# A home per quarter for the projection weight, late weights' pieces behind the normalised heads, and the last rows' slices dealt out anew

## The chip, the cores and the metric

One core of a Trainium2 chip runs one program of some 27,700 instructions. The metric is device time in microseconds (us), the median over the runs. The engines are TensorE (PE; its weight loads are shown as PEld), VectorE (DVE), ScalarE (ACT), GpSimd (POOL) and SyncE (SP), which issues the transfers (DMA).

## The reference, cut to what matters

Two transformer layers over 16 sequences of 128 rows and 512 features. The stretch that the change touches is the second layer's attention and the passage from it to the last feed-forward part.

```
def _L1_xattn_ref(hidden_states, cond, ...):      # 16 query heads, 8 key/value heads of 128
    ln_out = _ln(hidden_states, ln_w, ln_b)
    q  = _ln(_fp8_linear_pertensor(ln_out, wq, ...).reshape(b, s, g, hpg, d), ...)
    k  = _ln(_fp8_linear_pertensor(ln_out, wk, ...).reshape(b, s, g, d), ...)
    v  = _fp8_linear_pertensor(ln_out, wv, ...).reshape(b, s, g, d)
    core = _gqa(q, k, v).reshape(b, s, nh * d)
    qx = _ln(_fp8_linear_pertensor(ln_out, wqx, ...), ...)
    kx, vx = jnp.split(jnp.einsum('bsi,oi->bso', cond, w_kv_x), 2, axis=-1)
    xout = _gqa(qx, _ln(kx, ...), vx).reshape(b, s, nh * d)
    catq = _div_clamp_fp8(jnp.concatenate([core, xout], axis=-1), proj_smooth)
    return jnp.einsum('bsi,oi->bso', catq, wproj) * (proj_in_scale * proj_w_scale)

x = x + jnp.tanh(g_xattn[1]) * _L1_xattn_ref(_layernorm(x), ctx_2048, ...)
x = x + jnp.tanh(g_ffn[1]) * _L1_ffn_ref(_layernorm(x), ...)
```

## The kernel before

The attention of the second layer is a software pipeline of 64 tiles: four quarters of the heads (4 query heads, 4 cross query heads, 2 + 2 key and value heads) times 16 sequences (B = 16). Tile m belongs to quarter m // 16. All engines walk the same steps i from 0 to 63 (`step(i, par, quarter)`), each in its own fixed order, and meet by semaphores. A step does the projections of tile i + 1, the turning, scores and maxima around tile i, the softmax and the attention of tile i - 1, the fp8 rounding of tile i - 2 and the output projection of tile i - 3. Most steps of quarters 2 and 3 run in a hardware loop; the others are written out, so that extra work can be placed in them by number.

TensorE in a step: `keys_values` (L2517, L2518), `context_keys_values` (L99 to L101), `turn_probs` (L2589), half of the output projection with the weight `wp` (L2603), `turn` of the normalised heads (L2568), the other half, `attend`, `scores` (L2579; its second half waits until the residual of tile i - 3 has been added, since both use bank 5) and `queries`.

VectorE in a step: `maxima` (L2875), `probabilities` (L2882, L2884), the sums of squares (L2835), the first half of the fp8 rounding (L1299 to L1303), `normalise_b` (L2839, heads that TensorE then turns), `probs_low` (L2857), `sums_a` (L2831), the second rounding half, `residual` (L2898), `values_low` (L2847), `normalise_a`. ScalarE: exponentials (L2734), squares, probabilities out, `heads_out` (L2755 to L2761), `values` (L2717), `scaled_out` (L2772). GpSimd makes the reciprocal roots (L2482) between the sums of squares and `normalise_b`.

Three side jobs ride on the steps.

The **projection weight** of a quarter (8 x 512 columns) comes as fp32 to a spare slot and is cast to fp16 on ScalarE in four pieces (L2680, `wproj_part`) in step 16q + 2. There is one home for it (`wp`, 8 KB at 122 KB), so the first cast waits until the quarter before has done its last output.

The **late weights**: of the four quarters' projection weights, eight slices are centred and split into high and low parts while attention runs. Slice n is summed and centred on VectorE in step 8 + 3n (an opened step: `late.sums` L233, `late.means` L240, `late.centre_heads` L248), its high parts are made on ScalarE in the next step (L257, L261), its low parts on VectorE in the one after (a split step: `late.lo_segs` L269, `late.lo_plain` L274). SP loads two slices in step 7, after all of the last rows' slices are rounded, and one more with each that is done:

```
            if i == LATE_FIRST - 1:
                sp.wait_ge(sh.q_in, C * KT)
                late.load(sp, 0)
                late.load(sp, 1)
```

The **last rows**: the normalised rows of the last four sequences still have to be scaled on ScalarE (16 pieces, L1696, `rows_part`, dealt out by `ROW_PIECES`) and rounded on VectorE in four slices of 2048 columns (L1810 to L1816, `sh.rounded`), each at the end of the step after the one that `LAST_ROWS` names; SP then stores the slice (L1882).

Of the kernel before, what the change touches and what calls it, by code (L numbers as in the profile page):

```python
# [16 lines left out]
F32R = mybir.dt.float32r  # L17
# [8 lines left out]
P = 128  # L26
B = 16
# [1858 lines left out]
class Dense:  # L1886
# [10 lines left out]
    def __init__(self, nc, env, ctx, mem, home, late, wp_in, a_ps, e_in, x_in, mhalf):  # L1897
# [3 lines left out]
        def at(name, kb, shape, dt=FP32):  # L1901
            return mem.at("d_" + name, kb, shape, dt)
# [3 lines left out]
        for name, hi, lo, n in (("gate1", 149, 147, P), ("up", spare, spare + 8, D), ("down", 139, 131, D),  # L1906
                                ("expert", kv, kv + 8, D)):
            self.raw[name] = at("raw_" + name, lo, [P, KT, n])
            self.w[name] = [at(f"{name}_hi", hi, [P, KT, n], F32R), at(f"{name}_lo", lo, [P, KT, n], F32R)]
        self.hi, self.lo = ([at(f"xT_{n}{c}", kb + 8 * i, [P, KT, CW], F32R) for c, kb in enumerate((kvx, wq, wqx, 64))]  # L1910
                            for i, n in enumerate(("hi", "lo")))
        even = at("xn0", 151, [P, J, D])
# [361 lines left out]
def attention(nc, env, ctx, mem, ready, late, sh):  # L2274
# [10 lines left out]
    def sb(name, kb, shape, dt=FP32):  # L2285
        return mem.at(n_ + name, kb, shape, dt)
# [17 lines left out]
    cq = [sb(f"cq{i}", 118 + 2 * i, [P, KH, P], F16) for i in range(2)]  # L2304
    wp = sb("wp", 122, [P, 8, D], F16)
    c_hi = sb("c_hi", 164, [P, KT, P], F32R)
# [25 lines left out]

    LAST_ROWS = (1, 3, 4, 5)
    ROW_PIECES = {1: range(0, 3), 2: range(3, 4), 3: range(4, 6), 4: range(6, 9), 5: range(9, 12), 6: range(12, 16)}
    de = Dense(nc, env, ctx, mem, homes[Q - 1], late, wp_in, a_ps, e_in, x_in, mhalf)
# [174 lines left out]
    def tensor(pe):  # L2510
# [89 lines left out]

        def output_heads(par, heads):
            for h in heads:
                last = nc.tensor.matmul(bank[5][:], cq[par][:, h, :], wp[:, h, :], start=h == 0, stop=h == KH - 1)  # L2603
            return last

        def output_begin(m, par, read, quarter):
            if opens(m):
                pe.wait_ge(wp_in, m // B * 2 + 2)
            pe.wait_ge(cq_in, m * 2 + 2)
            pe.wait_ge(ex_in, read)  # L2610
            if later(m, 1):
                pe.wait_ge(x_in, m)
            output_heads(par, range(QH))

        def output_end(m, par):
            output_heads(par, range(QH, KH)).then_inc(pj_ps, 1)

        def output(m, par, read, quarter):
            output_begin(m, par, read, quarter)
            output_end(m, par)  # L2620

        def step(i, par, quarter):
# [9 lines left out]
            if has(i - 3):  # L2632
                output_end(i - 3, 1 - par)
            if has(i - 1):
# [37 lines left out]
    def scalar(act):  # L2672
        def wproj(quarter, part):
            i, a = divmod(part, 2)
            if quarter and part == 0:
                act.wait_ge(pj_ps, quarter * B)
            if part == 0:
                act.wait_ge(wraw_in, quarter * 16 + 16)
            raw = slots32[homes[quarter][SPARE]]
            last = nc.scalar.activation(wp[:, 4 * i + 2 * a:4 * i + 2 * a + 2, :], raw[:, i, 2 * a:2 * a + 2, :], ACT.Copy)  # L2680
            if a:
                last.then_inc(wp_in, 1)
# [7 lines left out]
        def wproj_part(i, part):  # L2690
            if isinstance(i, int) and i % B == 2 and i < M:
                wproj(i // B, part)

# [134 lines left out]
    def vector(dve):  # L2828
# [71 lines left out]
        def step(i, par, quarter):  # L2900
# [15 lines left out]
            if number(i) == M - 2:  # L2916
                de.normalise(dve, 0, range(2, J))
            if opened is not None:
                late.means(dve, opened)
                late.centre_heads(dve, opened, 0)  # L2920
            if split is not None:
                late.lo_segs(dve, split, late.SEGS[2:4])
            if has(i):
# [3 lines left out]
            if has(i + 1):  # L2927
                sums_a(i + 1)
            if not later(i, 1):
                sh.rounded(dve, C - 2, KT - 1)  # L2930
# [261 lines left out]
```

## Time and profile before

| | us |
|---|---|
| median of three runs | 1635.4 (1634.8 to 1638.3) |
| profiled execution | 1630.85 |
| its span | 1629.1 |
| TensorE busy in the span | 1574.2 (97%) |
| VectorE, ScalarE, GpSimd busy | 1150.1, 1015.2, 486.0 |
| share of TensorE in the chain that ended last | 71% |

The span is the time from the first to the last instruction of one profiled execution. Durations in the rows come from this execution. Matmuls overlap one another, so a busy share near 100% says that there is no hole, not that the engine does all it could.

### The profile page before, as it was taken

How to read it: one execution, taken by the hardware profiler on the slowest of the kernel's cores; microseconds unless marked ns; L12 is line 12 of the kernel's file. 1: busy time of each engine (PE TensorE's matmuls, PEld its weight loads, DVE VectorE, ACT ScalarE, POOL GpSimd, SP SyncE). 2: the span in 40 equal slices, each digit the busy share in tenths (PEclk: the TensorE clock that was granted, in tenths of full speed). 3: DMA queues.
4: the chain of work that ended last, by engine and by line, in shares of the span. 5: the costliest groups of instructions: out<-in, count | busy, mean ns of one | idle time of the engine just before them, and what ended most of it. 6: DMA issues, size and time to landing. Idle time of an engine off the chain costs nothing.

```text
span 1629.1 us, 27708 instructions
## 1 busy us (share of the span) xinstructions
PE 1574.2 (97%) x9392; PEld 1221.4 (75%) x9392; DVE 1150.1 (71%) x2380; ACT 1015.2 (62%) x2855; POOL 486.0 (30%) x515
## 2 busy tenths in 40 slices
PE   7989979999998999999999999999999999999998
PEld 6878766666777767777777777777777777777887
DVE  6358865444997778888888887677777777898322
ACT  4354335553467877877878777777777777875100
POOL 1000222223524333443333443433443343420000
PEclk9999989999999999999999999999999999999999
DMA  8030648885663232364243353121152121110011
GB/s 304 27 109 28 229 167 271 274 270 175 215 228 124 75 135 79 101 237 143 81 136 99 106 199 116 46 77 58 46 201 66 46 109 58 46 39 7 22 38 39
DMA packets 75813, 196.62 MB, mean 121 GB/s; under 512 B 6896, under 2 KB 27376, under 8 KB 69168
## 3 DMA queue, kind: packets, MB, share of 16 engines
q1 hardware_dynamic: 70016, 176.50, 31.6%
q0 software_dynamic: 5680, 18.62, 3.9%
q8 instruction: 67, 1.10, 0.3%
q14 instruction: 50, 0.41, 0.1%
HBM read 147.12 MB, written 47.97 MB: 120 GB/s over the span
## 4 chain that ended last, share of the span: by engine, by line
PE 71%; DVE 8%; ACT 5%; DMA 1%; issue 1%; POOL 1%; SPq 0%; POOLq 0%; ACTq 0%; DVEq 0%
PE bank L2518 9%; PE bank L2517 9%; PE bank L99 8%; PE bank L101 8%; PE bank L100 8%; PE bank L2579 6%; PE bank L2603 5%; PE bank L2568 4%; PE bank L1423 4%; PE bank L1443 4%; PE bank L2589 3%; ACT t_sc L2734 2%; POOL t_rs L2482 1%; PE bank L1403 1%; DVE x_res L1782 1%
## 5 line engine op out<-in xcount | busy, mean ns | idle before, releaser
L2517 PE MATMUL bank<-t_half,t_xh 128*128 128x256 f16 (+1 forms) x1024 | 309.3, 326 | 0.7 <-DVE t_hn L2839 0.7
L2518 PE MATMUL bank<-t_half,t_xh 128*128 128x256 f16 (+1 forms) x1024 | 306.0, 326 | 0.0
L2479 POOL TENSOR_SCALAR t_ve<-t_ss 128x4 f32<-128x4 f32 (+1 forms) x128 | 25.6, 200 | 580.0 <-DVE t_ss L2835 554.4
L2734 ACT ACTIVATE t_sc<-bank,t_mx 128x128 f32<-128x128 f32 x512 | 180.1, 386 | 17.7 <-DVE t_mx L2875 13.1
L2839 DVE TENSOR_TENSOR t_hn<-bank,t_rs 128x256 f32<-128x256 f32 (+1 forms) x256 | 130.0, 549 | 63.4 <-POOL t_rs L2482 63.4
L2482 POOL TENSOR_TENSOR t_rs<-t_ve,t_mhalf 128x4 f32<-128x4 f32 (+1 forms) x128 | 171.0, 1336 | 10.7
L2517 PEld LDWEIGHTS bank<-t_half,t_xh 128*128 128x128 f16 x1024 | 100.3, 98 | 66.7 <-issue 1.4
L2518 PEld LDWEIGHTS bank<-t_half,t_xh 128*128 128x128 f16 x1024 | 100.2, 98 | 66.0
L2772 ACT ACTIVATE t_y<-bank,smooth 128x128 bf16<-128x128 f32 x512 | 139.3, 401 | 2.3 <-DVE t_cq L1303 2.3
L2603 PE MATMUL bank<-t_wp,t_cq 128*128 128x512 f16 x512 | 130.7, 379 | 0.0
L2579 PE MATMUL bank<-t_hT 128*128 128x128 f32 x1024 | 126.2, 276 | 2.7 <-ACT t_hT L2761 2.3
L2579 PEld LDWEIGHTS bank<-t_hT 128*128 128x128 f32 x1024 | 120.0, 192 | 3.8 <-ACT t_hT L2761 2.8
L2734 ACT ACTIVATION_READ_ACCUMULATOR t_sc<-bank,t_mx 128x1 f32 x512 | 115.4, 225 | 0.0
L2568 PE MATMUL bank<-ident,t_hn 128*128 128x128 f32 x768 | 98.3, 274 | 13.9 <-DVE t_hn L2839 13.8
L2568 PEld LDWEIGHTS bank<-ident,t_hn 128*128 128x128 f32 x768 | 87.3, 140 | 30.0 <-DVE t_hn L2839 18.2
L99 PE MATMUL bank<-t_slot,t_c_hi 128*128 128x512 f32 x256 | 106.3, 415 | 1.3 <-DVE x_res L1771 1.3
L101 PE MATMUL bank<-t_slot,t_c_lo 128*128 128x512 f32 x256 | 101.0, 394 | 0.0
L100 PE MATMUL bank<-t_slot,t_c_hi 128*128 128x512 f32 x256 | 99.6, 389 | 0.0
L2761 ACT ACTIVATE t_hT<-bank,q_wb 128x512 f32<-128x512 f32 x128 | 92.8, 782 | 10.3 <-PE bank L2568 10.2
L2470 POOL TENSOR_SCALAR t_c_hi<-t_cr 128x512 fp32r<-128x512 f32 x63 | 95.0, 1507 | 7.1 <-issue 1.4
L2710 ACT ACTIVATE t_sqk<-bank 128x256 f32<-128x256 f32 x64 | 25.3, 395 | 110.8 <-PE bank L101 110.8
L2884 DVE TENSOR_TENSOR t_sc<-t_sc,t_ri 128x512 f32<-128x512 f32 x128 | 88.5, 692 | 4.4
(355 smaller groups left out, 3878.7 us busy)
## 6 DMA issues: line engine op xcount, KB each, us to landing
t_xh<-xq_scratch SPq DMA_DIRECT2D x64, 512.0 KB, 3.5
t_cr<-in_ctxT_dram SPq DMA_DIRECT2D x64, 256.0 KB, 2.7
t_half<-w_half SPq DMA_DIRECT2D x12, 1024.0 KB, 7.6
y_rows<-s_y SPq DMA_DIRECT2D x39, 256.0 KB, 2.4
e_w<-in_w_units_dram SPq DMA_DIRECT2D x8, 1024.0 KB, 11.8
w_rows<-in_w_qkv_dram SPq DMA_DIRECT2D x8, 1024.0 KB, 5.6
xq_scratch<-z_xs SPq DMA_DIRECT2D x16, 512.0 KB, 3.3
t_slot<-w_plain SPq DMA_DIRECT2D x4, 2048.0 KB, 8.4
```

The lines of the kernel that those rows point to most:

```text
L99: nc.tensor.matmul(out, a_hi, b_hi, start=first, stop=False)
L100: nc.tensor.matmul(out, a_hi, b_lo, start=False, stop=False)
L101: return nc.tensor.matmul(out, a_lo, b_hi, start=False, stop=last)
L2482: nc.gpsimd.tensor_tensor(rs[:, lo:hi], ve[:, lo:hi], mhalf[:, lo:hi], ALU.pow).then_inc(rs_in, 1)
L2517: nc.tensor.matmul(out, rows[:, k, kind, :], w[0][:, k, a:b], start=k == 0, stop=False)
L2518: last = nc.tensor.matmul(out, rows[:, k, kind, :], w[1][:, k, a:b], start=False, stop=k == KT - 1)
L2568: last = nc.tensor.transpose(b3[out][:, n, :], hn[:, h, :], env.ident[:])
L2579: last = nc.tensor.matmul(b3[4 + part][:, h, :], hT[:, (1 - part) * QH + h, :], hT[:, KH + (1 - part) * QG + h // 2, :], start=True, stop= ...
L2603: last = nc.tensor.matmul(bank[5][:], cq[par][:, h, :], wp[:, h, :], start=h == 0, stop=h == KH - 1)
L2734: last = nc.scalar.activation(sc[:, h, :], b3[4 + part][:, n, :], ACT.Exp, bias=mx[:, h:h + 1], accum_out=sm[:, h:h + 1])
L2772: nc.scalar.activation(y[:, part, ramp(h)], b3[6 + part][:, h, :], ACT.Copy, scale=env.smooth8[:, n:n + 1]).then_inc(y_in, 1)
L2839: nc.vector.tensor_tensor(hn[:, lo:hi, :], b3[bk][:, 0:hi - lo, :], rs[:, lo:hi].unsqueeze(2).broadcast_to([P, hi - lo, P]), ALU.mult).the ...
```

## The change

The cast projection weight gets a home in each quarter: the upper half of that quarter's query weight slot, whose lower half alone is used by the fp16 weight. The low part of one of the last stage's inputs, which had lain in that upper half, moves to where `wp` was, another moves a little. The wait for the previous quarter's last output goes, and the four casts are done two by two in steps 16q + 1 and 16q + 2. The last rows' pieces are dealt out over steps 1 to 7 instead of 1 to 6, and their roundings end steps 3, 4, 6 and 7 instead of 2, 4, 5 and 6. On VectorE the late weights' means, first centring and second pair of low parts go behind the normalised heads, the low probabilities and `sums_a`.

```diff
-        self.hi, self.lo = ([at(f"xT_{n}{c}", kb + 8 * i, [P, KT, CW], F32R) for c, kb in enumerate((kvx, wq, wqx, 64))]
-                            for i, n in enumerate(("hi", "lo")))
+        self.hi = [at(f"xT_hi{c}", kb, [P, KT, CW], F32R) for c, kb in enumerate((kvx, wq, wqx, 64))]
+        self.lo = [at(f"xT_lo{c}", kb, [P, KT, CW], F32R) for c, kb in enumerate((kvx + 8, 122, wqx + 8, 72))]
...
-    wp = sb("wp", 122, [P, 8, D], F16)
...
-    LAST_ROWS = (1, 3, 4, 5)
-    ROW_PIECES = {1: range(0, 3), 2: range(3, 4), 3: range(4, 6), 4: range(6, 9), 5: range(9, 12), 6: range(12, 16)}
+    wp = [sb(f"wp{q}", SLOTS[homes[q][WQ_]] + 8, [P, 8, D], F16) for q in range(Q)]
+    LAST_ROWS = (2, 3, 5, 6)
+    ROW_PIECES = {1: range(0, 1), 2: range(1, 2), 3: range(2, 5), 4: range(5, 8), 5: range(8, 11), 6: range(11, 14),
+                  7: range(14, 16)}
...
-                last = nc.tensor.matmul(bank[5][:], cq[par][:, h, :], wp[:, h, :], start=h == 0, stop=h == KH - 1)
+                last = nc.tensor.matmul(bank[5][:], cq[par][:, h, :], wp[quarter_of(m, quarter)][:, h, :], start=h == 0,
+                                        stop=h == KH - 1)
...
-            if quarter and part == 0:
-                act.wait_ge(pj_ps, quarter * B)
             if part == 0:
                 act.wait_ge(wraw_in, quarter * 16 + 16)
...
         def wproj_part(i, part):
-            if isinstance(i, int) and i % B == 2 and i < M:
-                wproj(i // B, part)
+            if isinstance(i, int) and i % B in (1, 2) and i < M and part % 2 == 0:
+                wproj(i // B, 2 * (i % B - 1) + part // 2)
...
-            if opened is not None:
-                late.means(dve, opened)
-                late.centre_heads(dve, opened, 0)
-            if split is not None:
-                late.lo_segs(dve, split, late.SEGS[2:4])
             if has(i):
                 normalise_b(i)
             if has(i - 1):
                 probs_low(i - 1)
             if has(i + 1):
                 sums_a(i + 1)
+            if opened is not None:
+                late.means(dve, opened)
+                late.centre_heads(dve, opened, 0)
+            if split is not None:
+                late.lo_segs(dve, split, late.SEGS[2:4])
```

## Rows read from the trace of the kernel before

**Rows 1.** The page, busy us (share of the span) and instructions.
```profile
PE 1574.2 (97%) x9392; PEld 1221.4 (75%) x9392; DVE 1150.1 (71%) x2380; ACT 1015.2 (62%) x2855; POOL 486.0 (30%) x515
```

**Rows 2.** Timeline of TensorE, steps 42, 43: start, us, what, count, [idle before <-releaser].
```profile
1141.30 1.03 PE L2589 MATMUL bank<-ident,t_sc 128*128 128x128 f32 x8
...
1156.39 1.03 PE L2589 MATMUL bank<-ident,t_sc 128*128 128x128 f32 x8
```

**Rows 3.** Timeline of VectorE, an ordinary step.
```profile
1142.23 1.29 DVE L2839 TENSOR_TENSOR t_hn<-bank,t_rs 128x512 f32<-128x512 f32 x2 [1.28 <-POOL t_rs L2482]
```

**Rows 4.** Timeline of ScalarE, an ordinary step.
```profile
1146.83 0.47 ACT L2717 ACTIVATE t_vv<-bank,sigma 128x256 fp32r<-128x256 f32 x1 [0.80 <-PE bank L101]
...
1149.87 0.37 ACT L2734 ACTIVATE t_sc<-bank,t_mx 128x128 f32<-128x128 f32 x1 [0.23 <-DVE t_mx L2875]
```

**Rows 5.** Timeline of ScalarE, the casts behind the values in step 34.
```profile
1024.47 2.03 ACT L2680 ACTIVATE t_wp<-t_raw 128x1024 f16<-128x1024 f32 x2
...
1028.36 1.15 ACT L2680 ACTIVATE t_wp<-t_raw 128x1024 f16<-128x1024 f32 x1
1029.30 0.46 ACT L2734 ACTIVATE t_sc<-bank,t_mx 128x128 f32<-128x128 f32 x1
```

**Rows 6.** Timeline of TensorE, turned probabilities of steps 5, 6; 19, 20; 35, 36.
```profile
571.42 1.03 PE L2589 MATMUL bank<-ident,t_sc 128*128 128x128 f32 x8
...
588.21 1.03 PE L2589 MATMUL bank<-ident,t_sc 128*128 128x128 f32 x8
...
788.49 1.03 PE L2589 MATMUL bank<-ident,t_sc 128*128 128x128 f32 x8
...
806.58 1.03 PE L2589 MATMUL bank<-ident,t_sc 128*128 128x128 f32 x8
...
1033.38 1.03 PE L2589 MATMUL bank<-ident,t_sc 128*128 128x128 f32 x8
...
1050.74 1.03 PE L2589 MATMUL bank<-ident,t_sc 128*128 128x128 f32 x8
```

**Rows 7.** Timeline of VectorE, a slice of the last rows rounded, then the maxima.
```profile
564.04 0.68 DVE L1810 TENSOR_SCALAR z_y<-z_y 128x2048 f16<-128x2048 bf16 x1
...
566.09 1.28 DVE L2875 TENSOR_REDUCE t_mx<-bank 128x4 f32<-128x512 f32 x2
```

**Rows 8.** Timeline of SP's queue, the last slice's store and the first late loads.
```profile
599.81 0.37 SPq L1882 DMA_DIRECT2D xq_scratch<-z_xs  x1
...
602.26 1.16 SPq L141 DMA_DIRECT2D l_rows<-in_w_qkv_dram  x2
```

**Rows 9.** The tile of the late loads (1 MB each), issue to landing.
```profile
DMA to landing us min/median/max: 5.4/5.7/11.7
```

**Rows 10.** Timeline of VectorE, part of a split step and of the next, opened one.
```profile
742.49 0.87 DVE L269 SCALAR_TENSOR_TENSOR l_lo<-l_rows,wfac,l_hi 128x256 f16<-128x256 f32 x2
...
757.68 0.17 DVE L240 TENSOR_SCALAR w_hs<-w_hs 128x12 f32<-128x12 f32 x1
...
759.05 1.29 DVE L2839 TENSOR_TENSOR t_hn<-bank,t_rs 128x512 f32<-128x512 f32 x2
...
762.90 0.74 DVE L2898 SCALAR_TENSOR_TENSOR x_res<-bank,coef,x_res 128x512 f32<-128x512 f32 x1
...
764.52 0.48 DVE L2847 SCALAR_TENSOR_TENSOR t_vv_lo<-bank,sigma,t_vv 128x256 fp32r<-128x256 f32 x1 [0.28 <-ACT t_vv L2717]
```

**Rows 11.** Timeline of VectorE, the residual of step 7.
```profile
612.25 0.74 DVE L2898 SCALAR_TENSOR_TENSOR x_res<-bank,coef,x_res 128x512 f32<-128x512 f32 x1
```

**Rows 12.** Timeline of TensorE, the scores of steps 7 and 17.
```profile
612.06 2.21 PE L2579 MATMUL bank<-t_hT 128*128 128x128 f32 x16
...
763.54 1.95 PE L2579 MATMUL bank<-t_hT 128*128 128x128 f32 x16
```

**Rows 13.** Timeline of TensorE ahead of the routed part.
```profile
213.83 1.25 PE L1107 MATMUL bank<-r_at_slot,r_at_row 128*128 128x39 f16 x32 [3.67 <-DVE r_at_row L1225]
```

**Rows 14.** Busy time by windows: us, PE, PEld, DVE, ACT, POOL, clock, DMA share, GB/s.
```profile
212.10:225.80 13.70, 7.27 (x51) 5.88 (x52) 9.83 (x26) 4.54 (x8) 4.55 (x4) 0.50 0.27 77
```

More of the change, by code:

```diff
@@ L2599, in attend, with output_heads @@
                 last.then_inc(pv_ps, 1)
-        def output_heads(par, heads):
+        def output_heads(m, par, quarter, heads):
             for h in heads:
-                last = nc.tensor.matmul(bank[5][:], cq[par][:, h, :], wp[:, h, :], start=h == 0, stop=h == KH - 1)
+                last = nc.tensor.matmul(bank[5][:], cq[par][:, h, :], wp[quarter_of(m, quarter)][:, h, :], start=h == 0,
+                                        stop=h == KH - 1)
             return last
@@ L2612, in output_begin, with output_end @@
                 pe.wait_ge(x_in, m)
-            output_heads(par, range(QH))
-        def output_end(m, par):
-            output_heads(par, range(QH, KH)).then_inc(pj_ps, 1)
+            output_heads(m, par, quarter, range(QH))
+        def output_end(m, par, quarter):
+            output_heads(m, par, quarter, range(QH, KH)).then_inc(pj_ps, 1)
         def output(m, par, read, quarter):
             output_begin(m, par, read, quarter)
-            output_end(m, par)
+            output_end(m, par, quarter)
         def step(i, par, quarter):
@@ L2632, in step @@
             if has(i - 3):
-                output_end(i - 3, 1 - par)
+                output_end(i - 3, 1 - par, quarter)
             if has(i - 1):
@@ L2679, in wproj @@
             raw = slots32[homes[quarter][SPARE]]
-            last = nc.scalar.activation(wp[:, 4 * i + 2 * a:4 * i + 2 * a + 2, :], raw[:, i, 2 * a:2 * a + 2, :], ACT.Copy)
+            last = nc.scalar.activation(wp[quarter][:, 4 * i + 2 * a:4 * i + 2 * a + 2, :], raw[:, i, 2 * a:2 * a + 2, :],
+                                        ACT.Copy)
             if a:
```

## The prediction

> **What bounds the kernel now.** I read the page first: TensorE's share of busy time says whether anything else can matter [rows 1]. It is busy 97% of the span, so a cost of another engine counts only where it makes TensorE wait. Next the timeline of TensorE in the attention loop, one ordinary step. The reader is to use the start of the eight turned probabilities (L2589) as a mark, once per step: 15.09 us from mark to mark [rows 2], with no idle entry between. In the same step ScalarE stands idle 0.80 us before the values (L2717) and 0.23 us before the exponentials (L2734), and VectorE 1.28 us before the normalised heads (L2839) [rows 3, 4]. So an ordinary step is TensorE's own work, and every step longer than 15.09 us has lost the difference to a wait. Last I went through the marks of all 63 steps and looked up what each long one waited for. Three causes stand out. Steps that cast the projection weight: 17.35 us, and 18.09 us in quarter 1, where pieces of a late weight lie in the same step [rows 5, 6]. Steps after VectorE rounds a slice of the last rows (L1810 to L1816): 16.79 us [rows 6, 7]. The steps with late weights' pieces on VectorE are as long as ordinary ones, within 0.1 us.
>
> **The casts.** In step 34 ScalarE does one cast ahead of the values, in its 0.80 us of idle, and three behind them: two of 2.03 us together and one that is followed by the exponentials 0.94 us after its start [rows 5]. Three times 0.94 less the 0.23 us of idle is 2.6 us by which the exponentials come late, and TensorE's step is 17.35 - 15.09 = 2.26 us longer [rows 6]. So the chain exponentials, squares, norm, turned heads lets 0.34 us go by free. After the change each of two steps has one cast ahead of the values (free, as now) and one behind: 0.94 - 0.23 = 0.71 us late, less 0.34, is 0.37 us a step and 0.74 us a quarter. Quarters 2 and 3 gain 2.26 - 0.74 = 1.5 us each, 3.0 us. In quarter 1, step 17 will lie under a larger delay of VectorE (below) and cost nothing of its own; step 18 still holds five ScalarE pieces of the late weight, which use up part of the 0.80 us. Both casts could then count (2 x 0.94 - 0.23 - 0.34 = 1.3 us) or one (0.37); I take 1.1, since there the third of 3.00 us shows that most of the 0.80 us was gone. Gain 3.00 - 1.1 = 1.9 us. The wait for the previous quarter's last output goes and so does its reason; it was hidden by work on either side and is costed at nothing. The raw weight was loaded long before (no idle in front of the first cast now). Where the cast weight lies costs nothing: the same reads by the same 512 matmuls; nor do the two moved low parts of the last stage, whose instructions stay the same.
>
> **Quarter 0 and the last rows.** Now the casts and the first rounding share step 2, which is as long as a step with casts alone (three of that kind: steps 2, 34, 50); VectorE's 2.05 us of rounding hid under ScalarE's 2.6. Three more roundings, ending steps 4, 5 and 6, cost 16.79 - 15.09 = 1.70 us each. Sum 2.26 + 5.1 = 7.4 us. After, the four roundings end steps 3, 4, 6 and 7, each alone: 4 x 1.70 = 6.8; step 2 has two casts, 0.4; step 5 has a third slice behind the values, 0.1; step 1 swaps two slices for two longer casts, 0.4. Sum 7.7: a loss of 0.3 us. So spreading them wins nothing, for rounding costs by its place ahead of the maxima (566.09 instead of 564.04) and not by how full the step is.
>
> **The queue behind the last rounding.** In step 7 SP's queue waits for all sixteen slices (the wait on q_in) and then issues the first two late loads. Now the last rounding ends step 6 (its store is issued at 599.81), the loads go at 602.26, a whole step before VectorE sums them in step 8 [rows 8]. After, the last rounding ends step 7 itself. Call its end T. Store issued, then the load at T + 0.45; how long 1 MB takes behind a store of 512 KB is told by the landings of the late loads, 5.4 us at least, 5.7 in the median, 11.7 at most, the last for two issued together behind others [rows 9]. I take 5.7, so T + 6.15. VectorE goes from the rounding to the maxima (1.28 us, so to T + 1.2) and then, in step 8, to the sums, which wait for that load: a new stall of 4.9 us. Behind it on VectorE stand the probabilities, the sums of squares, the heads; TensorE waits for the turned probabilities and the heads. All 4.9 us count. Behind the wait in SP's queue stand the context and the rows of tile 10, which GpSimd and TensorE want only after the heads of step 8, themselves late; they cost nothing while the stall is there, and at most their own landing of some us if it weren't. Bounds: nothing, if the load were no later than the sums; 10.9 us with the longest landing.
> The Trainium skill (DMA: Bandwidth & Descriptors, Anatomy of one DMA) gives for its path some 2.0 us fixed and bytes by 436 GB/s, 4.4 us for 1 MB; by that the stall would be 3.6 us and not 4.9, and the sum 1.3 us less. No late load here was that short (5.4 us at least), so the row is used.
>
> **Late pieces behind the heads.** In an opened step (eight: 8, 11 to 29) the means and the first centring took 759.05 - 757.68 = 1.37 us in front of the heads, where VectorE otherwise idles 1.28 [rows 3, 10]. Moving them can thus bring at most 0.1 us. They go behind the sums (L2831), ahead of the second rounding and the residual (L2898). The residual now ends at 762.90 + 0.74 = 763.64; after, 1.37 later, 765.01. TensorE's scores start at 763.54 and their second half (from the ninth of 16, 0.9 us on) waits for that residual. Step 7 of now shows what a late residual costs: it ended at 612.25 + 0.74 = 612.99, 0.93 us after the scores' start, and they took 2.21 us instead of 1.95, 0.26 lost [rows 11, 12]. After the change it ends 1.47 us after their start, 0.54 later still: 0.26 + 0.54 = 0.8 us a step. The other path, values' low parts (0.28 us of idle left) to maxima, is 1.1 us late and costs some 0.7, at the same time; the larger counts. 8 x 0.8 = 6.4, and 0.5 more in step 8, where the heads themselves are late and the scores follow closer. In a split step (eight) 0.8 us of low parts (L269, 742.49) move likewise; with the residual 0.10 us behind the scores' start, as in the opened step, it would end at 0.9 and cost no more than 0.2 us; I take half of it and a little, 0.13 x 8 = 1.0 us. Bounds: 0 and the whole 1.37 and 0.8 us a step, 17 us.
>
> **Sum.** -3.0 - 1.9 + 0.3 + 4.9 + 6.9 + 1.0 = +8.2 us. The profiled execution took 1630.85 us (span 1629.1); with the change 1639.05. It lies 4.55 below the median of the three runs, 1635.4, so the median goes to **1643.6 us**, 0.5% slower.
>
> **Rivals.**
> A. The tail takes the move: the residual and the values' low parts have more room than step 7 shows. Sum without 7.9: +0.3 us, 1635.7. For it: VectorE still idles 1.28 us ahead of the heads in an ordinary step, so it isn't full. Against: 0.28 us of idle is all that is left before the values' low parts in an opened step.
> B. The late load is early enough, the rest as forecast: +3.3 us, 1638.7. It needs the wait on q_in to be met a step sooner; the program doesn't do that.
> C, the other side. TensorE has one slack against anything late on VectorE. At 3.6 us of it the moved pieces cost nothing and 1.3 of the 4.9 us of stall stay, -3.3 us, from where it is faster by over 0.2%; with all swallowed, -4.6 us, 1630.8. Against: a rounding 2.05 us late [rows 7] cost 1.70.
> D. TensorE's clock. In the stall of step 8 TensorE would stand idle for about 5 us in two parts. From 212.1 to 225.8 us the granted clock was 0.50, the 1.2 GHz level, after TensorE had begun a wait of 3.67 us at 210.2 [rows 13]; it was busy 7.27 us in that stretch [rows 14], of which half, 3.6 us, is the clock's. A wait of 2 to 3 us as in the cast steps never did it. If step 8 does, up to 3.6 us more: 1647.2.
> The rule of the Trainium skill (TensorE: Matmul & The Clock Gate, Part 1: The HAM clock gate) that an idle TensorE falls back to half its clock and that activity releases it speaks for D; the trace agrees at 212 us.
>
> **Numbers.** Forecast 0.60, A 0.12, B 0.08, C 0.12, D 0.08. The likeliest's own range, with the landing at 5 to 7 us and 0.5 to 1.1 us for an opened step, is 1640 to 1647. For 8 in 10 it goes down through A and part of C to 1634.5 and up through D to 1648.5. About 0.2% (3.3 us) is what a measurement of this kernel can tell from no change. Faster by more: C, 0.12. Within: A and half of B, 0.16. Slower: the rest, 0.72.
>
> **What would show it.** Right: marks of 15.5 us after steps 33, 34, 49 and 50; four of 16.8 or more around steps 3 to 8; an idle entry of nearly 5 us on VectorE before L233 in step 8, released by the DMA; marks near 15.9 us in each opened step with the scores stretched to 2.7 us. Wrong: opened steps that stay at 15.09 to 15.2 us, or sums in step 8 without idle in front. Most of the forecast hangs on two readings, that the scores' second half is held by the residual and that the queue's wait on q_in stands before the first late load.

## The result, and the profile after

The changed kernel took 1641.1 us (median of nine runs, 1640.0 to 1644.8) against 1633.7 (nine runs, 1632.7 to 1638.3) for the kernel before: a ratio of 1.0046, 95% interval 1.0034 to 1.0059. It is 0.5% slower, as forecast; 1643.6 was forecast. The profiled execution of each took 1641.12 and 1630.85 us, their spans are 1638.5 and 1629.1.

The page's busy line of the changed kernel, which answers to [rows 1]: TensorE's busy time grew by 5.9 us, VectorE's and ScalarE's work is the same.

```profile
PE 1580.1 (96%) x9392; PEld 1222.8 (75%) x9392; DVE 1148.4 (70%) x2380; ACT 1015.5 (62%) x2855; POOL 495.8 (30%) x515
```

The marks tell where. Mark k is the start of the turned probabilities in step k (L2589 before, L2590 now, since the attention's lines moved down by one). From the first to the last of the 64 marks the loop took 966.36 us before and 976.66 now, 10.30 more; behind the last mark both have 153.3 us left. The span grew by 9.3 only, because the first mark came 0.96 us earlier in this execution; the code ahead of it is the same, and the first mark lies between 508.5 and 513.6 us in the executions of this study. So the comparisons of intervals below go by the loop. What its marks give is the price in one execution; how the ratios over several runs stand to it is said ahead of the experiments.

The timeline of TensorE now: marks of steps 5 to 9, then 17 and 18, then two ordinary steps, then those of the casts in quarter 2 (answers to [rows 2, 6]).

```profile
570.67 1.04 PE L2590 MATMUL bank<-ident,t_sc 128*128 128x128 f32 x8
...
587.47 1.03 PE L2590 MATMUL bank<-ident,t_sc 128*128 128x128 f32 x8
...
602.68 1.03 PE L2590 MATMUL bank<-ident,t_sc 128*128 128x128 f32 x8
...
623.57 0.66 PE L2590 MATMUL bank<-ident,t_sc 128*128 128x128 f32 x4 [3.92 <-DVE t_sc L2885]
624.39 0.66 PE L2590 MATMUL bank<-ident,t_sc 128*128 128x128 f32 x4 [0.16 <-DVE t_sc L2885]
...
643.00 1.03 PE L2590 MATMUL bank<-ident,t_sc 128*128 128x128 f32 x8
...
766.38 1.03 PE L2590 MATMUL bank<-ident,t_sc 128*128 128x128 f32 x8
...
782.47 1.03 PE L2590 MATMUL bank<-ident,t_sc 128*128 128x128 f32 x8
...
1030.55 1.03 PE L2590 MATMUL bank<-ident,t_sc 128*128 128x128 f32 x8
...
1046.05 1.04 PE L2590 MATMUL bank<-ident,t_sc 128*128 128x128 f32 x8
...
1136.97 1.03 PE L2590 MATMUL bank<-ident,t_sc 128*128 128x128 f32 x8
...
1152.06 1.03 PE L2590 MATMUL bank<-ident,t_sc 128*128 128x128 f32 x8
```

An ordinary step still takes 15.09 us. From mark 7 to mark 9 lie 40.32 us where before there were 32.15, 8.2 more: that is most of the loss. Step 17, an opened one, takes 16.09 instead of 15.09.

Interval by interval, after minus before, the loop's 10.3 us are:

| intervals | what lies there | predicted | measured |
|---|---|---|---|
| 1 to 9 | casts of quarter 0, four roundings, stall, first opened step | +6.5 | +6.8 |
| seven opened steps, 11 to 29 | means, first centring behind the heads | +5.6 | +6.9 |
| seven split steps without step 19 | low parts behind the heads | +0.9 | +0.9 |
| 18 to 20 | casts of quarter 1 with a split step | -1.8 | -1.3 |
| 34 to 36 and 50 to 52 | casts of quarters 2 and 3 | -3.0 | -3.0 |

**Step 8.** The timelines of VectorE and of SP's queue (answers to [rows 7, 8]):

```profile
612.11 0.68 DVE L1810 TENSOR_SCALAR z_y<-z_y 128x2048 f16<-128x2048 bf16 x1
...
614.16 1.28 DVE L2876 TENSOR_REDUCE t_mx<-bank 128x4 f32<-128x512 f32 x2
620.89 1.81 DVE L233 TENSOR_REDUCE w_hs<-l_rows 128x8 f32<-128x1024 f32 x2 [5.45 <-DMA l_rows<-in_w_qkv_dram]
```

```profile
614.28 0.37 SPq L1882 DMA_DIRECT2D xq_scratch<-z_xs  x1
614.69 1.49 SPq L141 DMA_DIRECT2D l_rows<-in_w_qkv_dram  x2
```

The store goes out when the last rounding is done, the load 0.41 us behind it, and VectorE waits 5.45 us for it. TensorE then stands idle 3.92 us ahead of its mark. The same timeline of TensorE, turned heads and scores of step 5 (first three rows) and of step 8 (last three), and the windows around it (TensorE's busy time alone, clock, DMA share, GB/s):

```profile
574.33 1.25 PE L2569 MATMUL bank<-ident,t_hn 128*128 128x128 f32 x8 [1.32 <-DVE t_hn L2840]
575.42 1.03 PE L2604 MATMUL bank<-t_wp,t_cq 128*128 128x512 f16 x4
...
577.71 1.95 PE L2580 MATMUL bank<-t_hT 128*128 128x128 f32 x16
...
628.36 1.97 PE L2569 MATMUL bank<-ident,t_hn 128*128 128x128 f32 x8 [0.81 <-DVE t_hn L2840]
630.12 1.86 PE L2604 MATMUL bank<-t_wp,t_cq 128*128 128x512 f16 x4
...
633.24 1.95 PE L2580 MATMUL bank<-t_hT 128*128 128x128 f32 x16
```

```profile
616.00:624.00 8.00, 4.08 (x25) 1.00 1.00 373
624.00:632.00 8.00, 7.04 (x29) 0.57 0.08 31
```

Behind the idle stretch the granted clock is down (0.57 in the mean of the window, which is 0.50, the 1.2 GHz level, for most of it): the projection's four matmuls take 1.86 us instead of 1.03, and from the turned heads to the scores it is 4.88 us instead of 3.38. That is 1.5 us of clock. So 40.32 us less two ordinary steps (30.18) is 10.1: two roundings at 1.7 us, 1.5 us of clock, and 5.2 us of stall. It is rival D's mechanism, on top of the forecast's stall and at under half of its price. With the clock back at 1.00 in time, most of the 1.5 us would have been lost to the residual instead, as e8 below shows.

**An opened step.** VectorE and TensorE in step 17 (answers to [rows 10, 12]):

```profile
770.45 0.16 DVE L240 TENSOR_SCALAR w_hs<-w_hs 128x12 f32<-128x12 f32 x1
770.65 1.23 DVE L248 TENSOR_TENSOR l_rows<-l_rows,w_hs 128x1024 f32<-128x1024 f32 x1
...
772.65 0.75 DVE L2899 SCALAR_TENSOR_TENSOR x_res<-bank,coef,x_res 128x512 f32<-128x512 f32 x1
773.31 0.68 DVE L248 TENSOR_TENSOR l_rows<-l_rows,w_hs 128x512 f32<-128x512 f32 x1
773.91 0.48 DVE L2848 SCALAR_TENSOR_TENSOR t_vv_lo<-bank,sigma,t_vv 128x256 fp32r<-128x256 f32 x1
```

```profile
771.71 1.06 PE L2580 MATMUL bank<-t_hT 128*128 128x128 f32 x8
773.54 1.13 PE L2580 MATMUL bank<-t_hT 128*128 128x128 f32 x8 [0.77 <-DVE x_res L2899]
```

The residual ends at 773.40, 1.69 us behind the start of the scores (1.47 forecast), whose second half waits 0.77 us for it. VectorE has no idle left in front of the values' low parts either. The page's costliest groups sum it up for all steps (busy, mean ns, then idle in front and what ended most of it): TensorE's scores now wait 8.4 us in all (2.7 before), 6.1 of them for the residual.

```profile
L2580 PE MATMUL bank<-t_hT 128*128 128x128 f32 x1024 | 128.9, 277 | 8.4 <-DVE x_res L2899 6.1
```

### The profile page after: what moved, and what is told of

The parts are those of the page before. It is cut to its first block, busy times and chain, and to the rows that moved or that the text cites. A ratio compares the mean times of both kernels' runs of the same rounds, so it can differ in the third digit from the quotient of the medians.

```text
span 1638.5 us, 27705 instructions
## 1 busy us (share of the span) xinstructions
PE 1580.1 (96%) x9392; PEld 1222.8 (75%) x9392; DVE 1148.4 (70%) x2380; ACT 1015.5 (62%) x2855; POOL 495.8 (30%) x515
## 3 DMA queue, kind: packets, MB, share of 16 engines
q1 hardware_dynamic: 70016, 176.50, 31.4%
## 4 chain that ended last, share of the span: by engine, by line
PE 72%; DVE 9%; ACT 3%; issue 2%; POOL 2%; DMA 1%; SPq 0%; POOLq 0%; DVEq 0%; ACTq 0%
PE bank L2518 9%; PE bank L2519 9%; PE bank L99 9%; PE bank L101 8%; PE bank L100 8%; PE bank L2580 6%; PE bank L2604 5%; PE bank L1423 4%; PE bank L2569 4%; PE bank L1443 4%; PE bank L2590 2%; POOL t_rs L2483 1%; ACT t_sc L2735 1%; PE bank L1403 1%; DVE t_hn L2840 1%
## 5 line engine op out<-in xcount | busy, mean ns | idle before, releaser
L2480 POOL TENSOR_SCALAR t_ve<-t_ss 128x4 f32<-128x4 f32 (+1 forms) x128 | 34.2, 267 | 582.2 <-DVE t_ss L2836 555.2
```

## The experiments

All loops below are from first to last mark in each kernel's profiled execution; before has 966.36 us, the changed kernel 976.66. Ratios are to the kernel before on the same chip.

The two don't give the same sum. The loop of the changed kernel is longer by 10.3 us, the medians differ by 7.4; and for this pair and all experiments with a ratio but e9, the ratio is 0.17 to 0.26% better than the loops say, 3 to 4 us. All loops are held against one execution of the kernel before, which was 2.8 us faster than the median of its nine runs. Where its other executions lose more isn't shown. So a difference of intervals tells what a part costs where it stands, and the ratio what the kernel gains over several executions.

**The late pieces alone put back (e1).** From the changed kernel:

```diff
+            if opened is not None:
+                late.means(dve, opened)
+                late.centre_heads(dve, opened, 0)
+            if split is not None:
+                late.lo_segs(dve, split, late.SEGS[2:4])
             if has(i):
                 normalise_b(i)
...
                 sums_a(i + 1)
-            if opened is not None:
-                late.means(dve, opened)
-                late.centre_heads(dve, opened, 0)
-            if split is not None:
-                late.lo_segs(dve, split, late.SEGS[2:4])
```

> The changed kernel with one part undone: VectorE's means, first centring and second pair of low parts stand ahead of the normalised heads again. The loop, from the first to the last mark (turned probabilities), takes 966.4 us before and 976.7 after. Theory (the moved pieces hold the residual, and with it the scores' second half): opened steps fall from 16.1 to 15.1 us, split ones from 15.23 to 15.1; the stall of step 8 stays. Loop 968.3 us, 0.1 to 0.2% slower than before. Rival (the casts' new place or their two steps slow every later step, and the order on VectorE is free): loop stays at 976 to 977 us.

Measured: loop 966.8 us, ratio 0.9979 (0.9968 to 0.9991). The opened and split intervals from mark 10 on are back at 15.09 us. The move costs 9.8 us in all where 7.9 were forecast: 7.8 in the opened and split intervals of the table, 0.6 in those of quarter 1 and 1.6 from mark 7 to mark 9, less 0.2 over the other intervals. The stall is untouched (VectorE's timeline, step 8):

```profile
623.42 1.81 DVE L233 TENSOR_REDUCE w_hs<-l_rows 128x8 f32<-128x1024 f32 x2 [5.33 <-DMA l_rows<-in_w_qkv_dram]
```

In the changed kernel the 1.6 us were spent at the half clock. It fell here too (the turned probabilities behind the stall take 1.93 us), but was back up at the turned heads, and from them to the scores it is 3.4 us, as in an ordinary step. Marks 7 to 9 are 38.7 us apart: 30.18, two roundings at 1.7 and 5.1 of stall. The move did not make the half clock last longer: with the pieces behind the heads too, it lasted 3.4 us in e4 and e8, as here, and 6.8 in the changed kernel's execution. The expectation was missed on both counts, loop 966.8 for 968.3 us and a ratio of 0.2% faster where 0.1 to 0.2% slower stood; the first miss is the clock's 1.5 us.

Intervals 18 to 20 sum to 31.4 us here, 1.9 less than before: the casts of quarter 1 gained what was forecast (1.9), and in the changed kernel 0.6 of it goes to the late residual.

**The last rows' dealing alone put back (e2).**

```diff
-    LAST_ROWS = (2, 3, 5, 6)
-    ROW_PIECES = {1: range(0, 1), 2: range(1, 2), 3: range(2, 5), 4: range(5, 8), 5: range(8, 11), 6: range(11, 14),
-                  7: range(14, 16)}
+    LAST_ROWS = (1, 3, 4, 5)
+    ROW_PIECES = {1: range(0, 3), 2: range(3, 4), 3: range(4, 6), 4: range(6, 9), 5: range(9, 12), 6: range(12, 16)}
```

> The changed kernel with the last rows' slices dealt out as before (roundings end steps 2, 4, 5, 6). Theory (the last rounding at the end of step 7 holds the first late loads, VectorE stands 5.4 us idle for them, and TensorE's clock falls): the idle ahead of the first sums is gone, the clock stays at 1.00, step 8 costs 1.0 us as any opened step; loop 970.7 us instead of 976.7, 0.2 to 0.3% slower than before. Rival (the idle in step 8 is the transfer's own length beside other traffic, whatever the rounding's place): it stays within 1 us of 5.4 and the loop at 975 us or more.

Measured: loop 972.4 us, 1.7 us above the expectation, ratio 1.0012 (0.9998 to 1.0026), where 0.2 to 0.3% slower was expected. The stall is gone (no idle in front of L233), marks 7 to 9 are 32.7 us apart. The miss is in interval 2 to 3, 17.75 us: there the granted clock was 0.50 from 532.7 to 536.2 us in this execution, behind an idle of 2.28 us ahead of the turned heads of step 2; e3 below has the same work and an idle of 2.30 us there, kept its clock and took 16.26.

**The casts alone (e3).** The changed kernel with both of the other parts put back, by the two edits above.

> Only the homes and the casts over two steps; rows and late pieces as before. Theory (a cast ahead of the values is free, one behind costs 0.4 us): steps after 33 and 34 of 15.5 us each instead of 15.09 and 17.35, after 49 and 50 the same; after 18 some 16.2 instead of 18.1, since no moved piece makes the residual late; loop 961.3 us, 5 us under before, 0.3% faster. Rival (casts in another home read or written at a higher price): the steps keep 16.2 us or more and the loop stays above 964.

Measured: loop 962.7 us, ratio 0.9954 (0.9938 to 0.9971): this part alone makes the kernel faster. The 1.4 us above the expectation lie in interval 2 to 3 again, 16.26 us: a cast in step 1 beside three slices costs 1.7 us, beside one slice (the changed kernel) 0.3. So the lighter step 1 of the new dealing is worth 1.4 us to the casts, which neither the forecast nor this expectation had seen.

**The late pieces behind the residual (e4).** From the changed kernel:

```diff
-            if opened is not None:
-                late.means(dve, opened)
-                late.centre_heads(dve, opened, 0)
-            if split is not None:
-                late.lo_segs(dve, split, late.SEGS[2:4])
...
                 residual(i - 3, quarter)
+            if opened is not None:
+                late.means(dve, opened)
+                late.centre_heads(dve, opened, 0)
+            if split is not None:
+                late.lo_segs(dve, split, late.SEGS[2:4])
```

> The changed kernel with the late weights' pieces put one place further back: behind the residual and ahead of the low parts of the values, instead of behind the sums of squares and ahead of the rounding of the last rows and the residual. First theory: a piece behind the heads costs what it delays on VectorE up to the next operation for which TensorE waits, and in an opened step that is the residual, which ended 1.69 us behind the start of the scores. With the pieces behind it only the low parts of the values come late, so the opened intervals fall from 16.1 us to 15.1 to 15.8, the split ones stay at 15.1 to 15.2, the interval that holds step 19 falls from 16.8 to 16.3 us, and the loop from its first to its last mark is 970 to 974 us (976.7 in the changed kernel). Rival, that late work of VectorE anywhere behind the heads counts in full: opened intervals 16.0 to 16.1 and a loop of 976.7 us.

Measured: ratio 1.0033 (1.0018 to 1.0047), loop 975.0 us. The first theory, mine, fell. TensorE's timeline around opened step 17 (marks 17, 18, 19 and the scores between):

```profile
769.01 1.03 PE L2590 MATMUL bank<-ident,t_sc 128*128 128x128 f32 x8
...
774.45 1.95 PE L2580 MATMUL bank<-t_hT 128*128 128x128 f32 x16
...
784.21 1.03 PE L2590 MATMUL bank<-ident,t_sc 128*128 128x128 f32 x8
...
790.54 1.95 PE L2580 MATMUL bank<-t_hT 128*128 128x128 f32 x16
...
800.30 1.03 PE L2590 MATMUL bank<-ident,t_sc 128*128 128x128 f32 x8
```

The scores no longer wait (1.95 us), and the opened interval is 15.20; but the next one is 16.09. Together they are 1.0 us longer than in the kernel before, as in the changed kernel. The values' low parts, and with them the maxima, exponentials and next heads, are late in place of the residual. Of the 1.6 us that the loop is shorter than the changed kernel's, 0.4 lie between marks 7 and 10, where the half clock again ended ahead of the turned heads, 0.7 between marks 17 and 22 around the casts of quarter 1, and most of the rest in the split steps, which are back at 15.09 us.

**The late weights one step later (e5).** From the changed kernel:

```diff
-LATE_FIRST = 8
+LATE_FIRST = 9
```

> The changed kernel with the series of late weights begun one step later (step 9 in place of step 8), so that the first late loads are issued a step later than the last rounding of the last rows asks for. First theory, that the stall of step 8 is the first late load's wait for the last rounding plus its 5.4 us of transfer, and that the fall of TensorE's clock behind it is caused by that stall: the intervals from mark 7 to mark 9 fall from 40.3 us to 32.5 to 34 us, no stretch of half clock between the marks 7 and 10, the opened intervals stay 16.1 us and each comes one step later, the loop is 968 to 971 us. Rival, that the stall belongs to the last rows' slices themselves (their dealing over steps 3, 4, 6 and 7) and not to the late load: 38 us or more from mark 7 to mark 9 and a loop of 976 us.

Measured: ratio 1.000 (0.999 to 1.001), loop 969.9 us, 6.8 us shorter than the changed kernel's and still 3.5 longer than that of the kernel before. Marks 7 to 9 are 33.6 us apart, 6.7 less. The windows of TensorE there (its busy time, clock, DMA share, GB/s) have no half clock:

```profile
616.00:618.00 2.00, 2.00 (x11) 1.00 0.00 0
...
626.00:628.00 2.00, 0.95 (x7) 1.00 1.01 418
628.00:630.00 2.00, 2.00 (x16) 1.00 0.09 37
```

6.7 us is what was read off the changed kernel as 5.2 of stall and 1.5 of clock. Both are gone once the first late loads and sums come a step further behind the last rounding. The first opened step, now step 9, costs 0.7 us in interval 9 to 10.

**Both pieces dosed (e8).** From the changed kernel:

```diff
-                    late.lo_segs(dve, split, late.SEGS[0:2])
+                    late.lo_segs(dve, split, late.SEGS[0:1])
...
+            if opened is not None:
+                late.means(dve, opened)
             if has(i):
                 normalise_b(i)
...
             if opened is not None:
-                late.means(dve, opened)
                 late.centre_heads(dve, opened, 0)
             if split is not None:
-                late.lo_segs(dve, split, late.SEGS[2:4])
+                late.lo_segs(dve, split, late.SEGS[1:4])
```

> The changed kernel with two of the late weights' pieces shifted in opposite directions: in an opened step the 0.20 us of the means is issued ahead of the heads again, which leaves 1.14 us of centring behind them in place of 1.34; in a split step a further piece of 0.66 us follows behind the heads, which makes 1.44 us in place of 0.78. First theory, that behind the heads VectorE has a cover of about 0.4 us in an opened step and 0.65 us in a split one and every further microsecond is paid in full: opened intervals 15.85 to 15.9 us (16.05 to 16.10 in the changed kernel), split ones, with the interval behind them, together 0.6 to 0.7 us longer than the 30.3 us of the changed kernel, loop 979 to 981 us. Rival, that the price is a fixed one for having a piece there at all: opened 16.05 to 16.1 us, split 15.21 to 15.24 us, loop 976.7 us.

Measured, in one execution: loop 980.1 us. Opened 15.88 us, split 15.92. Seen on TensorE's timeline, marks 15 to 18:

```profile
739.97 1.03 PE L2590 MATMUL bank<-ident,t_sc 128*128 128x128 f32 x8
...
755.14 1.03 PE L2590 MATMUL bank<-ident,t_sc 128*128 128x128 f32 x8
...
771.06 1.03 PE L2590 MATMUL bank<-ident,t_sc 128*128 128x128 f32 x8
...
786.94 1.03 PE L2590 MATMUL bank<-ident,t_sc 128*128 128x128 f32 x8
```

0.20 us less of work behind the heads gave 0.20 us back, 0.66 us more cost 0.70: one for one, past a cover of about 0.4 us (opened) and 0.65 us (split). The rival of a fixed price is out.

This execution also tells what step 8 would have cost the changed kernel with the clock back in time. TensorE stood idle 4.03 us, the granted clock was 0.50 from 628.0 to 631.5 us, and the turned heads ran at 1.00. Then the scores had to wait for the residual:

```profile
635.36 1.06 PE L2580 MATMUL bank<-t_hT 128*128 128x128 f32 x8
637.10 1.13 PE L2580 MATMUL bank<-t_hT 128*128 128x128 f32 x8 [0.69 <-DVE x_res L2899]
```

From mark 8 to mark 10 it is 34.05 us here, 34.02 in e4 (where the loss falls in the second interval), 33.13 in e1, which has the pieces ahead of the heads, and 34.62 in the changed kernel. So with the half clock over in time the late pieces of step 8 cost 0.9 us (in e8 with 0.2 us less of them), and the longer half clock cost the changed kernel only 0.4 to 0.6 us more than they would have. The 1.5 us of clock stand in their place and are not added to them.

**The rounding elsewhere (e6).** e3 with the rounding of the last rows moved from the end of a step to behind the next step's maxima:

```diff
                 maxima(i - 1)
+                if number(i) - 2 in LAST_ROWS:
+                    sh.rounded(dve, C - 1, LAST_ROWS.index(i - 2))
...
-            if number(i) - 1 in LAST_ROWS:
-                sh.rounded(dve, C - 1, LAST_ROWS.index(i - 1))
```

> As the casts alone, and the four roundings of the last rows moved from the end of a step to just behind the next step's maxima, where VectorE otherwise waits 1.03 and 0.49 us for the exponentials. Theory (a rounding costs by its place ahead of the maxima): 2.05 us in 1.5 us of idle, at most 0.5 us late, so up to 0.3 us a step instead of 1.7; loop 956 us, 0.6% faster than before; the first late loads are issued some 4 us later than before and may make the sums of step 8 wait up to 1 us. Rival (the steps are long because VectorE is too full there): they keep 16.5 us or more, loop 961.

Measured: loop 957.8 us, ratio 0.9922 (0.9904 to 0.9939). The timeline of VectorE shows why:

```profile
582.38 1.28 DVE L2875 TENSOR_REDUCE t_mx<-bank 128x4 f32<-128x512 f32 x2
583.57 0.68 DVE L1810 TENSOR_SCALAR z_y<-z_y 128x2048 f16<-128x2048 bf16 x1
...
585.01 0.69 DVE L1816 TENSOR_SCALAR z_xs<-z_y 128x2048 int16<-128x2048 int16 x1
585.62 0.17 DVE L2882 RECIPROCAL t_ri<-t_sm 128x4 f32<-128x4 f32 x1
```

The rounding lies where VectorE would otherwise wait for ScalarE's exponentials, and steps of 16.8 us become 15.1 to 15.2. This shows the forecast's sentence that a rounding costs by its place and not by how full the step is, to hold. Intervals 7 to 9 kept 1.5 us of excess.

**Slices dealt lightly at first (e7).** e6 with

```diff
-    LAST_ROWS = (1, 3, 4, 5)
-    ROW_PIECES = {1: range(0, 3), 2: range(3, 4), 3: range(4, 6), 4: range(6, 9), 5: range(9, 12), 6: range(12, 16)}
+    LAST_ROWS = (2, 3, 4, 5)
+    ROW_PIECES = {1: range(0, 1), 2: range(1, 2), 3: range(2, 5), 4: range(5, 8), 5: range(8, 12), 6: range(12, 16)}
```

> The kernel of e6 (casts over two steps, pieces ahead of the heads, the last rows' rounding just behind the next step's maxima) with its slices dealt out with one in step 1, one in step 2, three, three, four and four in the steps 3 to 6, and the slices of the last rows rounded in the steps 4 to 7. First theory: what a step pays is the number of ScalarE's slices and casts in it ahead of what TensorE waits for; step 1 with one slice is paid as in the changed kernel (14.85 us in place of 16.25), four slices in a step cost no more than three, and the rounding stays out of the path: the loop is 956.0 to 957.5 us (957.8 in e6), ratio to the kernel before 0.991 to 0.992. Rival, that the slices taken out of step 1 are paid again where they go: a loop of 957.8 us or more.

Measured: 1625.4 us, loop 957.1 us, ratio 0.9922 (0.9905 to 0.9939). Interval 2 to 3 is 14.84, as expected, but a fourth slice in step 5 costs 0.7 us there (15.91), so half of the 1.4 us is paid again. Each theory was half right. The ratio can't be told from e6's.

**The late weights one step later again (e9).** e7 with e5's edit, `LATE_FIRST = 9`.

> The kernel of e7 with the late weights begun one step later (step 9). First theory, that the 0.9 us and 0.6 us by which the intervals 7 to 8 and 8 to 9 still exceed 15.1 us in e7 come from the context rows that stand behind the first late loads in the queues, in the same step as the last rounding: they fall to 15.1 to 15.2 us, and the second quarter's casts cost what they did (the intervals 17 to 20 together 46.3 to 46.6 us): loop 955.4 to 956.2 us against 957.1 in e7. Rival, that they belong to the last rounding itself or to the late loads wherever they are issued (the excess then moves a step on): loop 957.1 us or more.

Measured: loop 956.7 us, ratio 0.9945 (0.9927 to 0.9964). The loop lies under the rival's 957.1 us or more and over the first theory's 955.4 to 956.2. Intervals 7 to 8 and 8 to 9 stay at 16.03 and 15.73, with no excess moved a step on: the late loads have nothing to do with it. The timeline of GpSimd in e7 names the wait (2.66 us in e9):

```profile
603.08 0.20 POOL L2479 TENSOR_SCALAR t_ve<-t_ss 128x8 f32<-128x8 f32 x1 [9.37 <-DVE t_ss L2835]
603.37 1.64 POOL L2482 TENSOR_TENSOR t_rs<-t_ve,t_mhalf 128x8 f32<-128x8 f32 x1
607.49 1.62 POOL L2470 TENSOR_SCALAR t_c_hi<-t_cr 128x512 fp32r<-128x512 f32 x1 [2.48 <-DMA t_cr<-in_ctxT_dram]
```

**SyncE's stores a step later (e10).** e7 with

```diff
-            if i - 1 in LAST_ROWS:
-                sh.store(sp, (C - 1) * KT + LAST_ROWS.index(i - 1))
+            if i - 2 in LAST_ROWS:
+                sh.store(sp, (C - 1) * KT + LAST_ROWS.index(i - 2))
```

> The kernel of e7 with SyncE's stores of the last rows' slices issued one of its steps later, so that the store, which waits for the rounding, no longer stands ahead of the next context rows. First theory, that the excess over 15.1 us in the intervals 7 to 8 (15.98) and 8 to 9 (15.71) is the context row queued behind the store: GpSimd waited 2.48 us for it in e7 and VectorE 0.93 to 1.03 us for the reciprocal roots behind that. Both intervals fall to 15.1 to 15.3 us, the interval 6 to 7 (15.9, four slices in a step) stays, loop 955.4 to 956.0 us against 957.1 in e7, ratio to the kernel before about 0.990 to 0.994. Rival, that the context row is late because the queue or its transfers are taken by the other loads of that moment: GpSimd's wait stays over 1.5 us and the loop at 957.1 us.

Measured: 1621.0 us, loop 956.3, ratio 0.9916 (0.9900 to 0.9933), the lowest ratio of the study, though its interval overlaps those of e6 and e7. GpSimd's wait for the context row is gone:

```profile
601.22 1.64 POOL L2482 TENSOR_TENSOR t_rs<-t_ve,t_mhalf 128x8 f32<-128x8 f32 x1
602.94 1.50 POOL L2470 TENSOR_SCALAR t_c_hi<-t_cr 128x512 fp32r<-128x512 f32 x1
```

Interval 8 to 9 is back at 15.09. Interval 7 to 8 stays at 15.89, as long as 6 to 7: both belong to steps with four slices. The expectation (15.1 to 15.3) had put 0.6 to 0.8 us of it down to the queue too, and the loop is 0.3 us over its range.

## Why the prediction was right

**The casts.** Quarters 2 and 3: 1.50 and 1.51 us gained for 1.5 forecast each; the two steps take 15.49 and 15.45, so one cast behind the values costs 0.4. Quarter 1's casts are worth 1.9 us with the late pieces put back (e1), 1.9 forecast. In the changed kernel 0.6 of this is lost again, since the split step's late pieces hold the residual there. The forecast had costed the two parts one by one; here they share a step.

**Quarter 0 and the last rows.** Steps 3 to 7 came out as forecast: 15.51 for the step with two casts, 16.8 for each interval behind a rounding, 15.2 for the third slice. Interval 7 to 8 was 17.06 us before, not the 16.79 that the forecast took for every step behind a rounding; the 0.26 us of stretched scores in step 7, which it used elsewhere, were left out here. What the forecast also missed is that the new dealing does buy something: with the old one the cast of step 1 would have cost 1.7 us and not 0.3 (e3). "Spreading them wins nothing" is right against the kernel before, wrong for the two parts of the change together.

**The queue behind the last rounding.** Right in mechanism and nearly in size: 5.45 us of idle on VectorE and 5.2 on the loop for 4.9 forecast. The landing was the mis-sized number, 6.2 us and not 5.7. This is the row of the two first late loads in the changed kernel:

```profile
DMA to landing us min/median/max: 6.2/7.2/8.2
```

The figures of the Trainium skill (DMA: Bandwidth & Descriptors, Anatomy of one DMA), which it gives for transfers issued by GpSimd, would put a lone 1 MB at an estimated 4.4 us. SyncE issues these; this row, with 512 KB of store ahead and a second load beside it, is 1.8 us longer, and the measurement decides.

**TensorE's clock.** Forecast and rival D were set against each other, and they came together: the stall of 5.2 us, and 1.5 us of the up to 3.6 for the half clock. The granted clock fell behind an idle of 3.92 us, 3.81 in e1, 4.14 in e4, 4.03 in e8; without the stall (e5) it stayed at 1.00. Its upper bound had the half clock paid in full; here the part of it ahead of the turned heads lay where TensorE waited for VectorE anyway, and only the stretch from heads to scores was paid. The Trainium skill's rule that an idle TensorE drops to half its clock (TensorE: Matmul & The Clock Gate, Part 1: The HAM clock gate) agrees with these four. Rival D's remark that a wait of 2 to 3 us never did it held for that one execution of the kernel before; in e2 one of 2.28 us did.

**Late pieces behind the heads.** This is the step that was mis-sized: 0.98 us for each opened step where 0.8 stood; the split steps cost 0.13, as forecast. The residual ended 1.69 us behind the scores' start instead of 1.47. The forecast took VectorE's start in the opened step from the kernel before, but the split step ahead of it now leaves VectorE late as well: the maxima of step 17 began 7.38 us ahead of the mark before and 7.16 now, which is those 0.22 us. The model of one late operation, the residual, was also too narrow: e4 freed it and the same 1.0 us came from the values' low parts, whose cost the forecast had put at 0.7 and as covered by the residual's. Better is what e8 shows: past a cover of 0.4 to 0.65 us, work behind the heads is paid one for one. The extra 0.5 us in step 8 did not come: its scores ran without a break (1.95 us), for at half clock TensorE came to them late and the residual was ready. That was this execution's luck: in e4 and e8 the clock was back sooner and the pieces cost 0.9 us there.

**The sum.** Forecast +8.2 on the profiled execution; the loop lengthened by 10.3. The difference is about 1.3 from the opened steps, 1.5 of clock, 0.5 in quarter 1 and 0.3 of stall, less the 1.3 that step 8's residual did not cost and the 0.3 that step 7 had cost before. The profiled execution was forecast at 1639.05 us and took 1641.12. That the median comes out 2.5 us under the forecast all the same is luck, two misses of opposite sign. The second is the forecast's last term: 4.55 us were added from profiled execution to median, and the changed kernel's profiled execution is its median. The medians differ by 7.4 us, with the one before 1.7 lower over nine runs than over the three.

**Rivals A, B and C** are out: too little room in the tail (opened 16.1 us), the load late by 5.45, and no slack of 3.6 us or more, but 0.4 to 0.65 (e8).

## What to carry to other kernels

Where an engine waits in each step for another one, that idle time is the place for side work; the same work past the point where the chain leaves for the bounding engine costs, here beyond a cover of 0.4 to 0.65 us, its full length, in both places tried (ahead of the residual and behind it). Before a producer is moved by a step, look for queue waits on its count and for what stands behind them: here one late rounding cost a 5.2 us stall and the clock behind it, and a store waiting ahead of a context row cost another engine 2.5 us. Parts of a change should be timed alone: the casts alone made this kernel 0.5% faster, with the rounding in VectorE's idle time 0.8%, while all three parts together made it 0.5% slower.

## What the runs showed of the hardware

An idle of 3.8 to 4.1 us on TensorE within the loop was followed by a granted clock of 0.50 in all four executions that had one, for some 3.4 us in e1, e4 and e8 and 6.8 us in the changed kernel; the recurring idles of 1.3 us ahead of the turned heads in steps behind a rounding were not. Idles in between did it in some executions only. In e2 the clock fell for 3.4 us at 532.7 us, behind an idle of 2.28 us; idles of 2.30 us at the same place in e3 and e6 and one of 2.61 us in the kernel before left it at 1.00. Ahead of the loop it fell for 3.4 us behind idles of 1.7 us near 422 us (e1, e2) and of 1.8 to 2.3 us near 484 us (changed kernel, e3, e4, e9). Idles as long in the same places left it at 1.00 in other executions: 1.6 to 1.8 us near 422 us in e3, e4 and e6, 1.8 and 2.2 us near 483 us in e8 and e10. What decides it, and when the clock comes back, was not settled here.

The first mark came at 508.5 us in one execution and at 513.6 in another, with the same instructions ahead of it. These 5 us are 0.3% of the time, as much as some of the effects here, and none of it is the change's; counted from mark to mark, ordinary steps agree to 0.02 us between kernels.
